# Cross-attention in fp32 pieces: transposed inputs laid out on the host, and the bias row added by an accumulating DMA

## The reference

```
text_p  = x @ W_text + b_text              audio_p = ctx @ W_audio + b_audio
Q = layer_norm(text_p, g1, beta1)          K = layer_norm(audio_p, g2, beta2)      V = audio_p
alpha = softmax(Q @ K.T / sqrt(512))
H = (alpha @ V) @ W_out + b_out
out = layer_norm(H + x, g_out, beta_out)
```

## Time and profile before

| | before |
|---|---|
| median of 3 runs | 1487.2 us (1487.1 to 1487.49) |
| span of the profiled execution | 1486.0 us |
| TensorE busy | 1436.8 us, 97% |
| VectorE busy | 1147.9 us, 77% |
| GpSimd busy | 1050.5 us, 71% |
| ScalarE busy | 855.9 us, 58% |
| DMA moved | 121.44 MB, mean 82 GB/s |

### The profile page before, as it was taken

One profiled execution on the slowest core, in us unless ns is written; L12 is line 12 of the kernel. 1 busy time (PEld: TensorE's weight loads), 2 busy tenths in 40 slices (PEclk: granted clock), 3 DMA queues, 4 the chain that ended last, 5 costly groups with the idle time before them and its releaser, 6 DMA issues.

```text
span 1486.0 us, 26150 instructions
## 1 busy us (share of the span) xinstructions
PE 1436.8 (97%) x8240; PEld 1219.4 (82%) x8240; DVE 1147.9 (77%) x1657; ACT 855.9 (58%) x1547; POOL 1050.5 (71%) x1223
## 2 busy tenths in 40 slices
PE   8999999999999999999999999999999999999996
PEld 6788888888888888888888888888888888888885
DVE  6578777887777887777887778877778877788777
ACT  5465666555665555665556656556655466655563
POOL 2466777667867667776678676677776777766786
PEclk9999999999999999999999999999999999999999
DMA  5212221122221122211222211222212222112211
GB/s 191 71 43 86 100 99 53 67 85 92 99 99 46 66 90 93 99 67 53 85 92 99 99 49 64 92 92 99 84 43 78 92 99 99 51 67 87 93 50 58
DMA packets 63449, 121.44 MB, mean 82 GB/s; under 512 B 8385, under 2 KB 24769, under 8 KB 63425
## 3 DMA queue, kind: packets, MB, share of 16 engines
q1 hardware_dynamic: 63424, 121.14, 22.6%
HBM read 62.40 MB, written 33.55 MB: 65 GB/s over the span
## 4 chain that ended last, share of the span: by engine, by line
PE 33%; DVE 28%; POOL 23%; issue 12%; ACT 2%; DVEq 1%; SPq 1%; POOLq 0%; DMA 0%; ACTq 0%
POOL y_rows L901 8%; DVE qT_lo L663 8%; POOL y_rows L903 5%; DVE y_rows L685 5%; PE wide L255 5%; PE wide L253 5%; PE wide L254 5%; DVE q_cols L657 4%; PE turn L260 4%; DVE y_bn L690 3%; DVE row_max L700 3%; POOL squares L866 2%; DVE cT_lo L613 2%; POOL y_sc L859 2%; PE score L253 2%
## 5 line engine op out<-in xcount | busy, mean ns | idle before, releaser
L253 PE MATMUL wide<-xT_hi,wt_hi 128*128 128x512 f32 x512 | 209.9, 410 | 0.0
L255 PE MATMUL wide<-xT_hi,wt_lo 128*128 128x512 f32 x512 | 202.0, 395 | 0.0
L254 PE MATMUL wide<-xT_lo,wt_hi 128*128 128x512 f32 x512 | 201.9, 394 | 0.0
L895 POOL TENSOR_TENSOR y_rows<-x_in,bao_row 128x512 f32<-128x512 f32 x128 | 176.6, 1401 | 9.5 <-DVE bao_row L738 9.5
L507 ACT ACTIVATE qT_hi<-q_cols,beta_col 128x512 fp32r<-128x512 f32 x128 | 90.6, 725 | 154.7 <-DVE q_cols L657 154.7
L903 POOL TENSOR_TENSOR y_rows<-y_rows,betao_row 128x512 f32<-128x512 f32 x124 | 170.2, 1372 | 9.7
L901 POOL TENSOR_TENSOR y_rows<-y_rows,go_row 128x512 f32<-128x512 f32 x124 | 173.8, 1402 | 0.0
L657 DVE SCALAR_TENSOR_TENSOR k_cols<-k_cols,g_col,turn 128x512 f32<-128x512 f32 x128 | 89.6, 740 | 100.3 <-PE turn L260 100.3
L487 ACT ACTIVATE squares<-wide,btc_col 128x512 f32<-128x512 f32 x128 | 88.2, 689 | 135.4 <-PE wide L255 134.1
L857 POOL TENSOR_SCALAR y_sc<-y_mv 128x1 f32<-128x1 f32 x128 | 24.4, 191 | 192.6 <-DVE y_mv L695 187.2
L253 PE MATMUL wide<-cT_hi,wa_hi 128*128 128x512 f32 x384 | 159.3, 415 | 0.0
(11 more groups left out here) (116 smaller groups left out, 4081.1 us busy)
## 6 DMA issues: line engine op xcount, KB each, us to landing
x_in<-in_x SPq DMA_DIRECT2D x128, 256.0 KB, 4.3
out<-y_rows SPq DMA_DIRECT2D x128, 256.0 KB, 2.0
c_in<-in_ctx SPq DMA_DIRECT2D x32, 768.0 KB, 4.6
c_kept<-c_in SPq DMA_DIRECT2D x32, 768.0 KB, 3.5
q_cols<-in_L_xattn_W_text SPq DMA_DIRECT2D x1, 1024.0 KB, 5.6
y_rows<-in_L_xattn_W_out SPq DMA_DIRECT2D x1, 1024.0 KB, 8.1
k_cols<-in_L_xattn_W_audio SPq DMA_DIRECT2D x1, 768.0 KB, 4.7
bao_row<-in_L_xattn_b_out SPq DMA_DIRECT2D x1, 256.0 KB, 8.3
```

The lines of the kernel that those rows point to most:

```text
L253: nc.tensor.matmul(to, a_hi, b_hi, start=(m == 0), stop=False)
L254: nc.tensor.matmul(to, a_hi, b_lo, start=False, stop=False)
L255: done = nc.tensor.matmul(to, a_lo, b_hi, start=False, stop=(m == n - 1))
L895: nc.gpsimd.tensor_tensor(y_rows[odd][:, t, :], x_in[:, t, :], bao_row[:], ALU.add).then_inc(x_biased, 1)
```

## The change

Two things, in one diff. First, the host lays out x and the context twice, once as rows ([iteration, partition, tile, column]) and once transposed ([iteration, partition, block, token]), and the kernel loads the transposed form into `xT_in` and `cT_in`. The seven groups of transposes go, and `xT_high`, `cT_high` and the matching `low` read SBUF. The context rows are loaded straight into `c_kept`, the x rows straight into `y_rows`; the output is stored in the layout of the rows and turned back on the host.

Second, `bias_x` no longer adds on GpSimd. It waits for the x rows and issues one DMA on GpSimd's queue that adds `bao_row`, read four times over, to `y_rows`.

The order of SP's queue, in an iteration i, is then: stores of i-2 (tiles 2 and 3), context rows of i, transposed context of i+1, x rows of i (each tile behind its store of i-2), transposed x of i+1, stores of i-1 (tiles 0 and 1).

```diff
@@ SP @@
+            def load_cT(i):
+                sp.dma_start(cT_in[:], cT[i]).then_inc(cT_loaded, 16)
+
+            def load_xT(i):
+                sp.dma_start(xT_in[:], xT[i]).then_inc(xT_loaded, 16)
+
             def load_c(i):
-                sp.dma_start(c_in[:], c_v[i]).then_inc(c_loaded, 16)
-
-            def load_x(i, t):
-                sp.dma_start(x_in[:, t, :], x_v[i, :, t, :]).then_inc(x_loaded, 16)
+                sp.dma_start(c_kept[:], c_rows[i]).then_inc(c_loaded, 16)
+
+            def load_x(i, odd, t):
+                sp.dma_start(y_rows[odd][:, t, :], x_rows[i, :, t, :]).then_inc(x_loaded, 16)
...
                 if not first:
                     wait_apart(sp, c_split, T * i)
-                wait_apart(sp, c_loaded, 16 * (i + 1))
-                sp.dma_start(c_kept[:], c_in[:]).then_inc(c_copied, 16)
+                load_c(i)
                 if not last:
-                    wait_apart(sp, c_copied, 16 * (i + 1))
-                    wait_apart(sp, cT_done, CT * (i + 1))
-                    load_c(i + 1)
-                    wait_apart(sp, xT_done, DT * (i + 1))
-                    for t in range(T):
-                        wait_apart(sp, x_biased, T * i + t + 1)
-                        load_x(i + 1, t)
+                    wait_apart(sp, cT_split, CT * (i + 1))
+                    load_cT(i + 1)
+                if first:
+                    wait_apart(sp, xT_split, DT)
+                    load_xT(1)
+                    sp.wait_ge(wao_done, CT)
+                elif isinstance(i, int) and i == 1:
+                    sp.wait_ge(bao_done, 1)
+                for t in range(T):
+                    if not isinstance(i, int) or i >= 2:
+                        wait_apart(sp, stored[t], 16 * (i - 1))
+                    load_x(i, odd, t)
+                if not first and not last:
+                    wait_apart(sp, xT_split, DT * (i + 1))
+                    load_xT(i + 1)
...
@@ TensorE @@
                 project_k(i, 1)
                 if not first:
                     turn_p(j, 1)
-                    pe.wait_ge(pT_split, NB * j + 1)
-                turn_x(i, 0)
                 project_k(i, 2)
-                if not first:
-                    pe.wait_ge(pT_split, NB * j + 2)
-                turn_x(i, 1)
-                pe.wait_ge(xT_split, DT * i + 1)
-                turn_x(i, 2)
                 project_k(i, 3)
-                pe.wait_ge(xT_split, DT * i + 2)
-                turn_x(i, 3)
                 if first:
                     pe.wait_ge(wt_split, DT)
                 project_q(i, 0)
+                if not first:
+                    pe.wait_ge(pT_split, NB * j + 1)
                 turn_sum(i, turn[0], k_summed, k_sum_turned)
...
-                if not last:
-                    pe.wait_ge(k_normed, HT * (i + 1))
-                    turn_c(i + 1, 0)
-                    pe.wait_ge(q_normed, HT * (i + 1))
-                    turn_c(i + 1, 1)
                 pe.wait_ge(kT_split, HT * (i + 1))
                 scores(i, 0, 0)
-                if not last:
-                    pe.wait_ge(cT_split, CT * (i + 1) + 1)
-                    turn_c(i + 1, 2)
...
@@ ScalarE and VectorE @@
-                nc.scalar.copy(xT_hi[:, d, :], turn[d % 2][:]).then_inc(xT_hi_made, 1)
+                nc.scalar.copy(xT_hi[:, d, :], xT_in[:, d, :]).then_inc(xT_hi_made, 1)
...
-                low(xT_lo[:, d, :], turn[d % 2][:], xT_hi[:, d, :]).then_inc(xT_split, 1)
+                low(xT_lo[:, d, :], xT_in[:, d, :], xT_hi[:, d, :]).then_inc(xT_split, 1)
...
@@ GpSimd @@
-            def bias_x(i, odd, t):
-
-                if t == 0:
-                    pool.wait_ge(x_loaded, 16 * T * (i + 1))
-                wait(pool, stored[t], 16 * (i - 1))
-                nc.gpsimd.tensor_tensor(y_rows[odd][:, t, :], x_in[:, t, :], bao_row[:], ALU.add).then_inc(x_biased, 1)
+            def bias_x(i, odd):
+
+                wait_apart(pool, x_loaded, 16 * T * (i + 1))
+                wait_apart(pool, x_biased, 16 * i)
+                nc.gpsimd.dma_start(y_rows[odd][:], bao_row[:].rearrange("p (o h) -> p o h", o=1).broadcast_to([P, T, H]),
+                                    accum_op=ALU.add).then_inc(x_biased, 16)
...
                 row_rstd(i, k_ssq_made, k_ssq, k_ve, k_rs, k_var, k_rstd)
                 if not first:
-                    bias_x(i, odd, 0)
-                    bias_x(i, odd, 1)
+                    bias_x(i, odd)
                 pair_squares(i, q_squared, q_paired)
-                if not first:
-                    bias_x(i, odd, 2)
-                    bias_x(i, odd, 3)
                 row_rstd(i, q_ssq_made, q_ssq, q_ve, q_rs, q_var, q_rstd)
```

More of the change, by code:

```diff
@@ L76, in cross_attention_kernel @@
         g2_col, beta2_col = sb("g2_col", [P, HT]), sb("beta2_col", [P, HT])
-        x_in, c_in = sb("x_in", [P, T, D]), sb("c_in", [P, T, DC])
+        xT_in, cT_in = sb("xT_in", [P, DT, T * P]), sb("cT_in", [P, CT, T * P])
         c_kept = sb("c_kept", [P, T, DC])
@@ L203, in _ @@
             sp.dma_start(wt_stage[:], w_text.rearrange("(t p) h -> p t h", p=P)).then_inc(wt_loaded, 16)
-            for t in range(T):
-                load_x(0, t)
+            load_xT(0)
             sp.dma_start(wo_stage[:], w_out.rearrange("(t p) h -> p t h", p=P)).then_inc(wo_loaded, 16)
@@ L211, in store_y @@
                 wait_apart(sp, y_ready, T * j + t + 1)
-                sp.dma_start(out_v[j, :, t, :], y_rows[odd][:, t, :]).then_inc(stored[t], 16)
+                sp.dma_start(out[j, :, t, :], y_rows[odd][:, t, :]).then_inc(stored[t], 16)
             def step(i, odd, first=False, last=False):
@@ L238, in _ @@
                 sp.wait_ge(last_ready[by], count)
-                sp.dma_start(out_v[N - 1, :, t, :], y_rows[1][:, t, :]).then_inc(stored[t], 16)
+                sp.dma_start(out[N - 1, :, t, :], y_rows[1][:, t, :]).then_inc(stored[t], 16)
             for t in range(T):
@@ L277, in project_q @@
                 product(wide[h][:], terms, xT_split if h == 0 else None, DT * i).then_inc(q_done, 1)
-            def turn_x(i, d):
-                if d == 0:
-                    pe.wait_ge(x_loaded, 16 * T * (i + 1))
-                transposes(turn[d % 2], [x_in[:, t, d * P:(d + 1) * P] for t in range(T)]).then_inc(xT_done, 1)
-            def turn_c(i, d):
-                to = score[1] if d == 2 and isinstance(i, int) and i == 0 else turn[d % 2]
-                if d == 0:
-                    pe.wait_ge(c_loaded, 16 * (i + 1))
-                transposes(to, [c_in[:, t, d * P:(d + 1) * P] for t in range(T)]).then_inc(cT_done, 1)
             def turn_sum(i, to, summed, turned):
@@ L367, in _ @@
                 transposes(wide[h], [wa_stage[:, d, h * P:(h + 1) * P] for d in range(CT)]).then_inc(waT_done, 1)
-            for d in range(CT):
-                turn_c(0, d)
             pe.wait_ge(columns_loaded, 16 * 6)
@@ L616, in xT_low @@
                 dve.wait_ge(xT_hi_made, DT * i + d + 1)
-                low(xT_lo[:, d, :], turn[d % 2][:], xT_hi[:, d, :]).then_inc(xT_split, 1)
+                low(xT_lo[:, d, :], xT_in[:, d, :], xT_hi[:, d, :]).then_inc(xT_split, 1)
             def cT_low(i, d):
                 dve.wait_ge(cT_hi_made, CT * i + d + 1)
-                of = score[1] if d == 2 and isinstance(i, int) and i == 0 else turn[d % 2]
-                low(cT_lo[:, d, :], of[:], cT_hi[:, d, :]).then_inc(cT_split, 1)
+                low(cT_lo[:, d, :], cT_in[:, d, :], cT_hi[:, d, :]).then_inc(cT_split, 1)
             def pT_low(j, b):
@@ L942, in step @@
                     pool.wait_ge(wao_done, CT)
-                    for t in range(T):
-                        bias_x(i, odd, t)
+                    bias_x(i, odd)
                 for t in range(T):
```

54 lines of the change are left out of this document (30 added, 24 removed).

## The result

The changed kernel takes 1710.4 us (median of four runs, 1704.6 to 1717.6) where the kernel before takes 1487.35 us: a ratio of 1.150 with an interval of 1.147 to 1.153. It is 15% slower. The profiled execution spans 1715.7 us, so its steps are a little longer than those of the median run.

The account below looks back on a forecast made before the run. A four-piece ring through GpSimd, VectorE, TensorE and ScalarE, matched by TensorE's work, bounds the 45.22 us step. Forecast 15.5 + 14.5 + 4.0 + 18.1 = 52.1 us; 1487.2 + 207 - 4 = 1690 us, range 1600 to 1810.

Parts of the forecast that it names:

- (1): From the end of the exponentials to the older iteration's last finish_y: 13.0 us, forecast 15.5 by strict alternation at the port.
- the ring: The step's repeating chain of four pieces: 45.22 us before, forecast 52.1; removing the transposes was taken as worth 0.
- Rival C: The load waits as forecast but the port is shared mildly: 49.3 us a step, 1606 us; chance 0.15.
- T1 to T2: TensorE's way from the first (T1) to the second (T2) turn of square_sum: 12.9 us in the prediction.
- (2): From the last finish_y to square_sum's second turn: 10.4 us, forecast 14.5 as a serial chain behind the x rows' load.
- (3): From the second turn of square_sum to the turn of q_rs, TensorE's work: 4.0 us, forecast 4.0.
- rival E: TensorE's clock falls towards 1.2 GHz after long waits in (1): 1840 us; chance 0.08.
- (4): From the turn of q_rs to the next end of the exponentials, mostly VectorE: 17.8 us, forecast 18.1.
- lower variant, 1648 us: A GpSimd issue of 0.5 or issue-and-landing share of 1.3 us lets TensorE's way decide: 1.4 us a step less.
- A: TensorE is the bound after all, so every step loses 3.5 us: 1375 us, faster; chance 0.07.
- B: Neither the port nor the load bites and the old ring stays: about 1483 to 1487 us; chance 0.05.
- D: GpSimd's DMA issue is as dear as the additions were: 4.1 us more a step, 1813 us; chance 0.10.

Follow-up runs that it names:

- e8: Kernel before, transposes kept, with x rows also loaded into y_rows and the bias DMA behind row_rstd of q: 1483.05 us, 0.9953.
- e1: Changed kernel with the wait for x rows and the bias DMA moved behind row_rstd of q: 1603.2 us, 1.0760.
- e7: e1 plus 20 matmuls a step in TensorE's waits, whose results nobody reads: 1557.5 us, 1.0455.
- e4: Kernel before, transposes kept, with x rows also loaded into y_rows and the bias DMA where the changed kernel has it: 1627.4 us, 1.0925.
- e11: e8 with the order of e5 on GpSimd and SP, inputs still turned on TensorE: 1467.3 us, 0.9867.
- e5: Changed kernel, older finish_y of tiles 2, 3 behind row_rstd of k and pair_squares of q, DMA behind split_c, SP reordered: 1448.75 us, 0.9725.
- e9: e5 with finish_y of tile 1 moved behind row_rstd of k too: 1501.1 us, 1.0074.
- e3: Changed kernel with the next iteration's transposed x load issued only when the x rows have landed: 1691.1 us, 1.1362.
- e6: e5 with four GpSimd additions in place of the bias DMA: 1511.4 us, 1.0146.

## Why the forecast was right, and where its terms were off

**The parts.** Through the runs in steps, each with one edit: from 1487.35 the DMA in the old kernel, at the late place, is 4.3 less (e8; 7 by the ratio to its own runs of before); the transposed inputs 120 more (e8 to e1); the DMA put in front of `pair_squares` 107 more (e1 to the changed kernel), which makes 1710.4. Of the 120, 46 are the clock's (e7), which fell because TensorE waited in (1). In the other order the DMA's place costs 144 us (e8 to e4) and the inputs 83 (e4 to the changed kernel): the later the first turn of `square_sum`, the more of the wait for the x rows is hidden beside it. The forecast had put the removed transposes beside the ring. e8 against e1 agrees with it, since TensorE's work goes away and the step grows from 44.83 to 49.24, but it holds their worth and the port's price together. So does e11 against e5, in the other order, and there the two together are worth 0.5 us a step of the transposes' 3.5.

**Piece (1), the port: forecast 15.5, measured 14.33.** The mechanism was right and its size off. The strict alternation is there, but a turn costs GpSimd less than the 0.65 us I put. Starts of `finish_y`'s operations in the alternation are 1.82, 1.57 and 1.79 us apart (744.63, 746.45, 748.02, 749.81), against 1.38 and 1.25 with VectorE away: 0.3 to 0.4 a turn. VectorE bears the greater part, 0.68 grown to 1.75. The Trainium skill, page "SBUF — State Buffer", section "Who interferes with whom", says that a VectorE instruction with two SBUF inputs contends with a GpSimd instruction that reads SBUF; this trace agrees (1524 ns for an `xT_lo` with both operands in SBUF, 683 in e8 with one in PSUM). That SBUF operands are slow by themselves is excluded by e9: there both are in SBUF too, no `finish_y` runs beside them, and an `xT_lo` takes 686. Rival C, a port shared mildly, would have left `xT_lo` at 0.68; it is out, though its 49.3 us a step is where e1, without the load's wait, stands (49.24), for other reasons: the port in (1) and the clock in T1 to T2.

**Piece (2), the load: forecast 14.5, measured 16.79.** The chain is the one forecast, link by link. GpSimd waits 8.49 us in the step shown and 8.0 on average, where some 10 were named. By the step shown: SP 0.9 (forecast 0.9); loads 11.5 (8.7 with issue and landing); the GpSimd issue holds the queue 0.9, from 763.85 to 764.75 (1.5); the VectorE and GpSimd work behind 3.8 (3.4), since `pair_squares` is recorded with 1.77 right behind the DMA issue and with 1.28 elsewhere. These last two terms belong together: from the issue's start to the end of `pair_squares` it is 2.67 us, and the issue's 1.36 and a usual 1.28 make 2.64. The mis-sized term is the transfer. I took 391 GB/s from a window of the start; here the loads run at 359 to 364 GB/s once under way and at 261 in their first window, and `xT_in`, which I costed at nothing as a load that comes a stage early, takes its share: about 0.5 us a step, by e3. With nothing behind them the loads still took 10.1 us to land in e3's step. The Trainium skill, page "DMA: Bandwidth & Descriptors", section "Anatomy of one DMA — SWDGE (gpsimd) path", has a fit, made for one DMA of GpSimd's queue, by which these bytes would take 8.0 us (an estimate from that page); for these six DMAs on SP's queue the measured 10.1 decides.

**Piece (3): forecast 4.0, measured 5.20.** TensorE had waited before T2, and the clock was 0.67 in the window that holds it. I had left this to rival E. **Rival E** is half true: the clock falls in each step, both behind (1) and behind T2. It was priced at 150 us on top of the forecast. In the changed kernel the loss behind (1) hides beside the load, and what shows is (3), 1.2 us a step or some 36 us (in e4 too (3) is long, at 5.55, with the inputs turned on TensorE); in e1, where TensorE's way decides, it is 46 (e7).

**Piece (4): forecast 18.1, measured 16.75.** Wrong in sign. `cT_lo` was to cost 0.3 us more and takes 673 ns (668 before): beside it GpSimd has only short operations. And the stretch became shorter: `neg_max` took 913 ns on average and takes 600, since its first one no longer meets a `finish_y` of GpSimd, and `qT_lo` takes 1022 instead of 1096. By the groups of both traces that is (64 x 0.313 + 128 x 0.074) / 32 = 0.9 us a step, nearly the whole 1.0.

**The sum.** 52.1 forecast against 53.06: errors of -1.2, +2.3, +1.2 and -1.35. They cancel to 1 us. 1690 was 20 us low; that it came nearer than its terms were is luck. The prediction's lower variant, 1648 us, was also reckoned wrongly: a GpSimd issue of 0.5 us takes 1.0 from the load's chain and a landing share of 1.3 takes 0.7, and either alone is less than the 1.4 by which the load was ahead; only both together hand the decision to TensorE's way.

**The signs.** `xT_lo` at 1.2 us or more came (1.52). `finish_y`'s operations were to take 1.7 to 1.9 us and took 1.61 to 1.74 in the alternation; TensorE's share was to be near 80% and is 85%; both turns of `square_sum` were to wait for microseconds, and in the step shown they wait 0.74 and 2.70.

**Rivals.** A (TensorE the bound, 1375) and B (no bite) are out. D, a dear issue, is out: 1.37 us by the page of the profile.

**My expectations** left the clock out in e1 (28 us missed) and e4 (77). Those of e3 (46), e6 (76, with the 44 of e5 in it) and e9 (71 above the upper end of its first theory, 36 above that of its second) missed by as much: `xT_in` takes a smaller share than I put, the additions cost twice as much in (4), and the meeting in the q stage stood in no theory. For e5 (44), e9 shows what held E to T1: the one `finish_y` left in the k stage.

**Open.** Why some steps of the changed kernel take 51.1 and some 54.8 us was not tried; the clock granted differs between them. Nor was it tried whether SP's order alone is worth something (e5 and e11 have it together with GpSimd's), or the new order with the old inputs and the additions.

## What to carry to other kernels

A busy share of 97% did not make TensorE's work worth removing: find the ring first, then ask what of the removed work stands in it. When a PSUM operand becomes an SBUF one, look at what GpSimd does at that time: here every two-SBUF operation of VectorE that stood between two of `finish_y` went from 0.68 to about 1.75 us; and when additions become a DMA, put its wait behind everything that the ring needs from that queue. Once the order of the queues followed them, the same edits gave 1448.7 us instead of 1710.4.

## What the runs showed of the hardware

TensorE's clock fell to its lower level in the middle of a kernel, behind stretches in which it was partly busy (e1: 1.29 of 3 us at 1.00, then 1.65 of 3 at 0.55 and 1.95 of 3 at 0.50), and was still there while it was fully busy again (756 to 759, clock 0.50). Twenty useless products a step gave back 46 us (e7).

GpSimd's accumulating DMA, 1 MB within SBUF with the source read four times over, shows as 1.37 us and lands after 8.0 us (9.5 in e4). The next operation is recorded as starting after 0.9 us, but it then shows about 0.5 us more than elsewhere: `pair_squares` 1.77 to 1.79 instead of 1.28 (changed kernel and e4), `c_hi` 1.02 instead of 0.51 (e1). Since the addition is the same for both, I read it as an overlap of the records and not as slower work: the issue takes some 1.4 us of GpSimd.

In the alternation at the port the loser's time is not symmetric: VectorE's 0.68 us grew to between 1.75 and 1.79 (changed kernel and e9), GpSimd's 1.28 to between 1.61 and 1.74.
